# A graph layer's row gathers on GpSimd, issued in bursts of six that wait for TensorE's half groups

## The chip, the cores and the metric

The kernel is one program on one NeuronCore of a Trainium2 chip. The metric is the device time of one execution in microseconds (us); the time before is 13074.31 us, the median of three runs (13063.61 to 13083.32).

## The reference

The program computes nine layers on 32 sequences of 242 tokens with 64 features: a windowed token mixer, four attention layers and four feed-forward layers. The change touches only the last one, the graph layer, which treats all 7744 tokens as nodes of a graph with 262144 edges plus one loop per node:

```
h = (x_flat @ W_gat).reshape(M, HEADS, NUM_EXPERTS)      # 4 heads x 4 experts
a_src = (h * att_src).sum(-1); a_dst = (h * att_dst).sum(-1)
e = leaky_relu(a_src[src] + a_dst[dst], 0.2)
ee = exp(e - segment_max(e, dst)[dst])
alpha = ee / (segment_sum(ee, dst)[dst] + 1e-16)
agg = segment_sum(h[src] * alpha, dst) + b_gat
# layer norm, mean over heads, top 2 of 4 experts, and
out = sum over experts of gate * (gelu(x @ W1 + b1) @ W2 + b2)
```

What matters here is `h[src]` and `a_src[src]`: each of the 262144 edges needs the 20-number row (80 bytes) of its source node.

## The kernel before

In an earlier layer the edges are sorted by target node, so that each of the 128 partitions holds 2048 consecutive edges. The stage in question works through them in 16 chunks of `W = 128` edges per partition. For the edges of a chunk there are two ways to get the source rows:

- **Gathered.** The first `FETCHED = 72` edges of each partition come by indirect DMA: GpSimd issues one gather per edge column, 128 rows of 80 bytes each, from the table in device memory into `g_got` (L2829). That is 72 gathers per chunk and 1152 in all. Chunk `i` writes buffer `i % 3`.
- **Looked up.** The other 56 edges come in seven groups of eight by matrix products. ScalarE starts the DMA that lays the node numbers out (L2932), VectorE turns them into one-hot matrices (`mark`, L3001 and L3002), TensorE multiplies them with the table (`look`, L2861, in two halves of 24 matrix products), VectorE masks the product (`clear`, L3009, "g_picked"), TensorE folds it (`fold`, L2874) and ScalarE copies the rows out (`take`, L2954).

There are therefore 16 x 7 = 112 lookup groups, numbered G; the chunk is G // 7. TensorE does, for each G, the first half of the look of G, then the fold of G - 1, then the second half of the look of G. Two of its steps raise the semaphore `tensor_step` (looked up and folded): the fold of G brings it to 2G + 2, the second half of the look of G to 2G + 1. So it goes up by one per half of a group. VectorE's `clear` waits for the look, ScalarE's `take` for the fold, TensorE's fold for `clear`, and the look of G for the masking of G - 2. Also on TensorE in the same order are the small expert layers (L2838, L2845, L2854), two sequences per chunk, and before a fold in two of seven groups it waits for ScalarE's copy L2937.

VectorE's work on the finished rows of a chunk (`messages`) is cut into five pieces. From G = 16 on, one piece stands behind each group. The pieces of chunk `i` run, once the start is over, at G = 7(i + 1) + 1 to 7(i + 1) + 5. The second piece waits for the chunk's gathers (L3077), the fourth (L3095, "msg") reads `g_got` for the last time.

GpSimd's order is written out in one loop over chunks (L2811). Before chunk `i >= 3` it waits until VectorE's "msg" of chunk `i - 3` has freed the buffer, and then issues all 72 gathers in a run. In chunk 0 two other pieces of work stand between the gathers: 62 gathers of sorted keys (L2822), each waiting for a buffer that VectorE counts (L3026), ahead of gather 24, and 61 scatters of head values (L2827) ahead of gather 40. Chunks 1 and 2 wait for nothing.

Of the kernel before, what the change touches and what calls it, by code (L numbers as in the profile page):

```python
# [33 lines left out]
class Chain:  # L34
# [14 lines left out]
    def after(self, i, name):  # L49

        return i * self.per + self.end[name]
# [2442 lines left out]
def stage_l3_ffn(nc, h, xn, k, A):  # L2494
# [30 lines left out]
    with ExitStack() as outer:  # L2525
# [8 lines left out]
        with ExitStack() as edges:  # L2534
# [213 lines left out]
            PER = 7  # L2748
            MADE = GROUP * PER
            FETCHED = W - MADE  # L2750
            GROUPS = CHUNKS * PER
            with ExitStack() as ctx:
# [41 lines left out]
                vector_step, tensor_step, taken = sem("marked_and_cleared"), sem("looked_up_and_folded"), sem("rows_taken")  # L2794
# [3 lines left out]
                ch = Chain([sem("step")], ["fill", "weighed", "alpha", "sum", "leaky", "top", "diff", "gone", "fade", "exp", "msg", "run"])  # L2798
                s, after = ch.sem[0], ch.after
                SEARCH, SCATTER = 24, 40  # L2800
                PIECES, FIRST = 5, 2 * PER + 2
                slots, at_piece = [[] for _ in range(GROUPS)], 0
                for G in range(GROUPS):
# [5 lines left out]
                with nc.Block() as block:  # L2809
                    @block.gpsimd  # L2810
                    def _(g):  # L2811
                        for i in range(CHUNKS):
                            c = i % SLOTS
                            if i >= SLOTS:
                                g.wait_ge(s, after(i - SLOTS, "msg"))
                            for w in range(FETCHED):
                                if (i, w) == (0, SEARCH):
                                    g.wait_ge(ps_, pl("block_i"))
                                    for t in range(NODES + 1):
                                        if t >= RING:  # L2820
                                            g.wait_ge(near_used, t - RING + 1)
                                        g.indirect_dma_start(near[t % RING], None, ordered.rearrange("(n w) -> n w", w=BLK), bass.IndirectOffsetOnAxis(  # L2822
                                            ap=blk[:, t:t + 1].bitcast(U32), axis=0)).then_inc(near_in[t % RING], 16)
                                if (i, w) == (0, SCATTER):
                                    g.wait_ge(ps_, pl("place_i"))
                                    for t in range(NODES):
                                        g.indirect_dma_start(heads_at, bass.IndirectOffsetOnAxis(ap=place_i[:, t:t + 1].bitcast(U32), axis=0),  # L2827
                                                             brow[:, t, :], None).then_inc(heads_out, 16)
                                g.indirect_dma_start(got[c][:, w, :], None, rows, bass.IndirectOffsetOnAxis(  # L2829
                                    ap=idx[:, i * W + w:i * W + w + 1].bitcast(U32), axis=0)).then_inc(gathered[c], 16)  # L2830
# [679 lines left out]
```

## Time and profile before

| | |
|---|---|
| median of three runs | 13074.31 us |
| profiled execution, first to last instruction | 13092.4 us |
| TensorE busy | 10580.0 us (81%) |
| VectorE busy | 8992.0 us (69%) |
| ScalarE busy | 5348.0 us (41%) |
| GpSimd busy | 1494.4 us (11%), of it 1149.0 us in the 1152 gathers |
| TensorE's mean granted clock | 0.886 of full speed |

No other time of the profiled execution is given than its span; the profile has no time around it. Shares are means over nine very different layers, so they say little of one stage. The 112 lookup groups lie from about 10000 us to 12886 us of the span. A row of a timeline gives the start, the length, the engine and the line, and in brackets how long the engine had been idle before it and what ended that; "issue" is idle time in which the engine waited for nothing that the profile shows, "remote" that the releaser is not told.

### The profile page before, as it was taken

Reading aid. Unit: us, or ns where it says so; the run is one execution under the profiler, and the core shown is the slowest. Engines: PE = TensorE matmul, PEld = TensorE weight load, DVE = VectorE, ACT = ScalarE, POOL = GpSimd, SP = SyncE. Lnnn points to the kernel's source line nnn. Section 1 sums busy time; section 2 is a strip of 40 time slices with the busy share of each in tenths; the row PEclk is TensorE's granted clock in tenths of the full one; section 3 lists DMA queues with packets and bytes.
Section 4 is the critical chain, followed back from the end, with each engine's and each line's share of the span. In section 5 each row is a group of like instructions: output and inputs, shape, how many; then the busy total and the mean of one; then the engine's idle time right before and its main releaser. Section 6 shows DMA issues by size and latency. Waiting matters only on the chain. (4 is left out here: it accounts for less than half of the span.)

```text
span 13092.4 us, 170810 instructions
## 1 busy us (share of the span) xinstructions
PE 10580.0 (81%) x48685; PEld 6876.2 (53%) x48685; DVE 8992.0 (69%) x31958; ACT 5348.0 (41%) x12854; POOL 1494.4 (11%) x1505
## 2 busy tenths in 40 slices
PE   2597799996694999999999999999896356666663
PEld 2486577774583555555555555555695133333331
DVE  7777687775676888888888888887666123333335
ACT  2364356563352555555555555555452000000000
POOL 0000000000000000000000000000001644543442
PEclk6798799997896999999999999999897677777776
DMA  0000012110001444344444444444002522322222
GB/s 5 11 1 6 27 47 61 51 56 3 2 1 30 99 103 98 98 103 98 98 103 98 98 103 98 98 103 99 28 1 63 41 34 39 48 39 34 41 42 65
DMA packets 511176, 744.96 MB, mean 57 GB/s; under 512 B 183149, under 2 KB 423246, under 8 KB 489577
## 3 DMA queue, kind: packets, MB, share of 16 engines
q1 hardware_dynamic: 398623, 601.80, 18.6%
q0 software_dynamic: 76960, 65.91, 4.0%
q10 hardware_dynamic: 34688, 66.66, 2.1%
q8 instruction: 387, 6.34, 0.2%
q14 instruction: 518, 4.24, 0.1%
HBM read 459.00 MB, written 84.54 MB: 42 GB/s over the span
## 5 line engine op out<-in xcount | busy, mean ns | idle before, releaser
L1849 PE MATMUL pm_out<-pm_w,pm_tab 128*128 128x484 f32 x8192 | 3997.3, 569 | 0.2 <-DVE pm_w L2093 0.2
L1954 ACT ACTIVATE pm_e<-pm_sums 128x484 f32<-128x484 f32 x4096 | 2316.2, 573 | 1375.1 <-PE pm_sums L1864 1342.9
L2093 DVE SCALAR_TENSOR_TENSOR pm_w<-pm_sums,pm_e 128x484 f32<-128x484 f32 x4096 | 2660.9, 651 | 85.3 <-ACT pm_e L1954 68.9
L1849 PEld LDWEIGHTS pm_out<-pm_w,pm_tab 128*128 128x128 f32 x8192 | 1558.7, 191 | 1008.9 <-issue 733.6
L1864 PE MATMUL pm_sums<-pm_mv,pm_pick 96*128 96x484 bf16 x4096 | 1508.9, 369 | 20.4 <-DMA pm_mv<-pm_parts 20.4
L3009 DVE TENSOR_TENSOR g_picked<-g_lookup,g_mask 128x1024 f32<-128x1024 f32 x112 | 137.1, 1224 | 1797.4 <-PE g_lookup L2861 1008.7
L2829 POOL DMA_INDIRECT g_got<-gat_sources,ed_idx x1152 | 1149.0, 997 | 1269.8 <-DVE g_msg L3095 912.8
L2861 PE MATMUL g_lookup<-g_onehot,ed_parts 121*128 121x512 bf16 x2688 | 710.9, 410 | 432.7 <-issue 391.5
L2861 PE MATMUL g_lookup<-h,ed_parts 121*128 121x512 bf16 x2688 | 693.9, 410 | 221.4 <-issue 218.8
L2954 ACT ACTIVATE g_got<-g_ps 128x128 f32<-128x128 f32 x112 | 31.0, 277 | 2044.5 <-PE g_ps L2874 794.7
L1864 PEld LDWEIGHTS pm_sums<-pm_mv,pm_pick 96*128 96x128 bf16 x4096 | 408.9, 100 | 650.2 <-issue 405.5
L2861 PEld LDWEIGHTS g_lookup<-g_onehot,ed_parts 121*128 121x128 bf16 x2688 | 272.4, 103 | 837.7 <-issue 545.3
L2874 PE MATMUL g_ps<-ed_folds,g_picked 128*128 128x16 f32 x1792 | 258.2, 279 | 467.0 <-issue 261.6
L114 POOL TENSOR_TENSOR xn<-h,s_st 121x1024 f32<-121x1024 f32 x1 | 2.9, 2938 | 5208.0 <-DVE s_st L95 5208.0
L2861 PEld LDWEIGHTS g_lookup<-h,ed_parts 121*128 121x128 bf16 x2688 | 276.6, 105 | 603.8 <-issue 349.7
L936 ACT ACTIVATE a_s<-a_ps,a_nmax,a_rms 121x121 f32<-121x121 f32 (+1 forms) x1024 | 459.0, 503 | 177.6 <-DVE a_nmax L1018 176.7
L2874 PEld LDWEIGHTS g_ps<-ed_folds,g_picked 128*128 128x128 f32 x1792 | 271.3, 226 | 477.1 <-issue 335.5
L2039 DVE MAX8 pm_srt<-pm_sim 121x8 f32<-121x64 f32 x2880 | 475.2, 214 | 5.2
L863 PEld LDWEIGHTS a_pv<-a_vs,a_pT 121*121 121x121 f32 x3072 | 407.9, 187 | 21.6 <-ACT a_pT L942 1.0
L854 PE MATMUL a_ps<-a_kd,a_y 128*121 128x121 f32 (+1 forms) x2048 | 404.1, 320 | 0.0
L863 PE MATMUL a_pv<-a_vs,a_pT 121*121 121x65 f32 x3072 | 386.3, 262 | 0.9 <-DVE a_acc L1034 0.9
L2042 DVE MATCH_REPLACE8 pm_sim<-pm_srt,pm_sim 121x64 f32<-121x64 f32 x1920 | 386.5, 211 | 0.0
(595 smaller groups left out, 19254.8 us busy)
## 6 DMA issues: line engine op xcount, KB each, us to landing
pm_tab<-in_L_ffn_tables SPq DMA_DIRECT2D x128, 2048.0 KB, 8.0
pm_mv<-pm_parts SPq DMA_DIRECT2D x3072, 60.5 KB, 2.4
g_spread_low<-gat_low_and_high_rows ACTq DMA_DIRECT2D x112, 512.0 KB
pm_gb<-pk_threshold_rows SPq DMA_DIRECT2D x128, 242.0 KB, 7.6
gat_running<-g_rec SPq DMA_DIRECT2D x16, 1536.0 KB
g_got<-gat_sources,ed_idx POOLq DMA_INDIRECT x1152
gat_bounce<-a_keys SPq DMA_DIRECT2D x70, 256.0 KB
gat_bounce<-a_keys POOLq DMA_DIRECT2D x70, 256.0 KB, 4.7
```

Of the source, the lines that this page charges most:

```text
L854: ins = pe.matmul(S[0:TP, n % 2, KEYS[t]], y[n % 2][:, t * TP:(t + 1) * TP], kd[c][:, 0:(t + 1) * TP], start=False, stop=(t == NT - 1))
L863: ins = pe.matmul(PV[0:TP, at:at + V1], pT[n % 2][:, b, :], vs[c][:, j, n, :], start=(j == 0), stop=(j == t))
L936: ins = a.activation(s[n % 2][:, KEYS[t]], S[0:TP, n % 2, KEYS[t]], ACT.Exp, bias=nmax[n % 2][:, t:t + 1], scale=rms[c][:, t, n:n + 1])
L1849: pe.matmul(out[:, hd % 2, 0:CHUNK], tab[hd % 2][:, t, :], w[:, t % NW, :], start=(t == 0), stop=(t == KT - 1)).then_inc(used, 1)
L1864: pe.matmul(sums[:, t % NB, 0:CHUNK], pick[:, t % 2, :], mv[hd % 2][:, t // 2, :], start=True, stop=True).then_inc(sums_ready, 1)
L1954: a.activation(e[:, t % NW, :], sums[:, t % NB, 0:CHUNK], ACT.Exp).then_inc(exp_ready, 1)
L2039: ins = v.max(srt[:, n // 2, n % 2, r8:r8 + 8], x)
L2042: ins = v.match_replace(x, srt[:, n // 2, n % 2, r8:r8 + 8], x, NEG)
L2093: v.scalar_tensor_tensor(out=w[:, t % NW, :], in0=sums[:, t % NB, 0:CHUNK], scalar=0.0, in1=e[:, t % NW, :], op0=ALU.is_gt, op1=ALU.mult). ...
L2829: g.indirect_dma_start(got[c][:, w, :], None, rows, bass.IndirectOffsetOnAxis(ap=idx[:, i * W + w:i * W + w + 1].bitcast(U32), axis=0)).th ...
L2861: ins = pe.matmul(lookup[G % 2][:, half, :], parts[q][:, l, :, :].rearrange("k f i -> k (f i)"), onehot[G % ONEHOTS][:, l, half * BANK:(ha ...
L2874: ins = pe.matmul(ps[:, 0, at:at + HE], picked[G % 2][:, w * 128:(w + 1) * 128], folds[:, 0:HE], start=True, stop=True)
```

## The change

GpSimd's run of 72 gathers is cut into 12 bursts of six (`BURST = 72 / 14` rounded up). From chunk 1 on, before burst `b` of chunk `i`, GpSimd waits until `tensor_step` is at least 14(i - 1) + b, that is, until TensorE is through `b` half groups of the chunk before. The wait for 0 (chunk 1, burst 0) is left out. The wait for the free buffer stays, and so do all other engines' programs.

```
@@ -2798,6 +2798,7 @@
                 s, after = ch.sem[0], ch.after
                 SEARCH, SCATTER = 24, 40
+                BURST = -(-FETCHED // (2 * PER))
                 PIECES, FIRST = 5, 2 * PER + 2
@@ -2814,6 +2815,10 @@
                             if i >= SLOTS:
                                 g.wait_ge(s, after(i - SLOTS, "msg"))
                             for w in range(FETCHED):
+                                if i and w % BURST == 0:
+                                    half = 2 * PER * (i - 1) + w // BURST
+                                    if half:
+                                        g.wait_ge(tensor_step, half)
                                 if (i, w) == (0, SEARCH):
```

## Rows read from the trace of the kernel before

**Rows 1.** Costliest groups of the page: busy us, mean ns | idle before, releaser.

```profile
L3009 DVE TENSOR_TENSOR g_picked<-g_lookup,g_mask 128x1024 f32<-128x1024 f32 x112 | 137.1, 1224 | 1797.4 <-PE g_lookup L2861 1008.7
L2829 POOL DMA_INDIRECT g_got<-gat_sources,ed_idx x1152 | 1149.0, 997 | 1269.8 <-DVE g_msg L3095 912.8
```

**Rows 2.** Stretches of the stage: us, busy of PE, PEld, DVE, ACT, POOL, clock, DMA.

```profile
10593.00:12883.00 2290.00, 1521.42 (x7126) 810.09 (x7124) 791.12 (x1633) 131.64 (x245) 935.49 (x936) 0.77 0.25 42
...
10593.00:10700.00 107.00, 107.00 (x590) 62.15 (x589) 51.14 (x104) 10.26 (x19) 0.00 (x0) 1.00 0.15 45
10269.00:10593.00 324.00, 73.97 (x214) 28.65 (x213) 15.19 (x32) 2.34 (x6) 222.69 (x228) 0.53 0.30 15
```

**Rows 3.** Slices of 12 us from the start of one run of gathers.

```profile
12095.00:12107.00 12.00, 12.00 (x70) 6.89 (x70) 7.46 (x18) 0.28 (x1) 9.53 (x9) 1.00 0.47 52
12107.00:12120.00 13.00, 12.51 (x67) 6.41 (x64) 4.87 (x13) 0.28 (x1) 9.98 (x10) 1.00 0.64 178
12120.00:12132.00 12.00, 3.13 (x13) 2.41 (x13) 4.07 (x9) 0.00 (x0) 9.26 (x10) 0.59 0.33 20
...
12168.00:12180.00 12.00, 2.34 (x4) 0.51 (x5) 0.00 (x0) 0.00 (x0) 9.08 (x10) 0.50 0.22 8
...
12204.00:12216.00 12.00, 12.00 (x66) 7.14 (x65) 4.78 (x10) 1.25 (x2) 0.00 (x0) 1.00 0.18 44
```

**Rows 4.** Timeline of GpSimd: first, slowest and last gather of that run.

```profile
12094.92 1.04 POOL L2829 DMA_INDIRECT g_got<-gat_sources,ed_idx  x1 [82.04 <-DVE g_msg L3095]
...
12130.85 2.07 POOL L2829 DMA_INDIRECT g_got<-gat_sources,ed_idx  x1 [0.30 <-issue]
...
12186.90 0.94 POOL L2829 DMA_INDIRECT g_got<-gat_sources,ed_idx  x1 [0.31 <-issue]
```

**Rows 5.** Timeline of TensorE before, in and after that run.

```profile
12076.21 3.57 PE L2874 MATMUL g_ps<-ed_folds,g_picked 128*128 128x16 f32 x16 [6.59 <-ACT ed_xT L2937]
12079.62 7.78 PE L2861 MATMUL g_lookup<-g_onehot,ed_parts 121*128 121x512 bf16 x24
...
12107.76 1.86 PE L2874 MATMUL g_ps<-ed_folds,g_picked 128*128 128x16 f32 x16
12109.47 5.34 PE L2861 MATMUL g_lookup<-g_onehot,ed_parts 121*128 121x512 bf16 x24
...
12129.07 2.31 PE L2874 MATMUL g_ps<-ed_folds,g_picked 128*128 128x16 f32 x10 [8.26 <-issue]
...
12164.20 0.58 PE L2861 MATMUL g_lookup<-h,ed_parts 121*128 121x512 bf16 x1 [2.21 <-issue]
```

**Rows 6.** Timeline: steps of VectorE and ScalarE that TensorE releases, in that run.

```profile
12101.14 1.22 DVE L3009 TENSOR_TENSOR g_picked<-g_lookup,g_mask 128x1024 f32<-128x1024 f32 x1 [4.41 <-issue]
...
12114.31 0.28 ACT L2954 ACTIVATE g_got<-g_ps 128x128 f32<-128x128 f32 x1 [18.09 <-remote]
...
12127.79 1.23 DVE L3009 TENSOR_TENSOR g_picked<-g_lookup,g_mask 128x1024 f32<-128x1024 f32 x1 [15.93 <-remote]
...
12196.45 0.28 ACT L2954 ACTIVATE g_got<-g_ps 128x128 f32<-128x128 f32 x1 [81.86 <-remote]
```

**Rows 7.** Timeline of VectorE: the picks of G = 11, 103, 110 and 111.

```profile
10593.33 1.22 DVE L3009 TENSOR_TENSOR g_picked<-g_lookup,g_mask 128x1024 f32<-128x1024 f32 x1 [51.11 <-PE g_lookup L2861]
...
12766.48 1.23 DVE L3009 TENSOR_TENSOR g_picked<-g_lookup,g_mask 128x1024 f32<-128x1024 f32 x1 [4.41 <-PE g_lookup L2861]
...
12868.86 1.23 DVE L3009 TENSOR_TENSOR g_picked<-g_lookup,g_mask 128x1024 f32<-128x1024 f32 x1 [4.40 <-PE g_lookup L2861]
...
12882.57 1.22 DVE L3009 TENSOR_TENSOR g_picked<-g_lookup,g_mask 128x1024 f32<-128x1024 f32 x1 [6.78 <-PE g_lookup L2861]
```

**Rows 8.** Stretches within the first run of 72: until and from its first late step.

```profile
10705.00:10744.00 39.00, 39.00 (x214) 22.14 (x212) 28.67 (x63) 2.34 (x6) 30.39 (x26) 1.00 0.43 101
10744.00:10802.00 58.00, 19.30 (x64) 7.42 (x63) 8.13 (x18) 1.56 (x2) 44.25 (x46) 0.58 0.23 17
```

**Rows 9.** Timeline at the end of the longest run: last gather, ScalarE's next step.

```profile
10559.88 1.00 POOL L2829 DMA_INDIRECT g_got<-gat_sources,ed_idx  x1 [0.30 <-issue]
...
10588.37 0.28 ACT L2954 ACTIVATE g_got<-g_ps 128x128 f32<-128x128 f32 x1 [47.91 <-remote]
```

**Rows 10.** The stretch of the paced key gathers.

```profile
10082.00:10204.00 122.00, 106.61 (x491) 58.96 (x492) 77.17 (x192) 6.25 (x14) 59.64 (x62) 0.86 0.52 164
```

**Rows 11.** Timeline of GpSimd: one pause among the key gathers.

```profile
10104.53 0.94 POOL L2822 DMA_INDIRECT g_rec<-gat_ordered,g_blk  x1 [4.64 <-DVE g_weighed L3026]
```

More of the change, by code:

```diff
@@ L2800, in stage_l3_ffn @@
                 SEARCH, SCATTER = 24, 40
+                BURST = -(-FETCHED // (2 * PER))
                 PIECES, FIRST = 5, 2 * PER + 2
@@ L2816, in _ @@
                             for w in range(FETCHED):
+                                if i and w % BURST == 0:
+                                    half = 2 * PER * (i - 1) + w // BURST
+                                    if half:
+                                        g.wait_ge(tensor_step, half)
                                 if (i, w) == (0, SEARCH):
```

## The prediction

> **What bounds the kernel now.** I read the page's costliest groups first, then stretches of the graph stage, then one run of gathers engine by engine. In the groups, VectorE's pick sits idle 1797.4 us before its 112 executions, mostly until TensorE's look, and GpSimd sits idle 912.8 us of its 1269.8 us before the gathers until "msg" frees a buffer [rows 1]. So GpSimd isn't short of time, and VectorE waits for TensorE. One would say that TensorE bounds the stage. But in the 2290 us from G = 11 to G = 111 it is busy only 1521.42 us, at 0.77 of its clock, while in the 107 us without a gather it is busy all the time at 1.00 [rows 2].
>
> The slices over one run of gathers show where the rest goes. Two slices after the run's start TensorE still executes 70 and 67 products; then 13, and further on 4 per slice, at clock 0.50; once the gathers are over, 66 again [rows 3]. The gathers go from 12094.92 to 12186.90 at an even step (0.94 us and 0.30 us of issue; 2.07 us was the slowest) [rows 4]. TensorE's rows say how it is slowed: a half group of 24 products takes 5.34 us, in the run single products come 2.8 us apart (0.58 and 2.21 of "issue") though nothing in the program stands between them [rows 5]. And what TensorE tells others comes late: the fold that ends at 12109.62 is acted on by ScalarE at 12114.31, the look that ends at 12114.81 is seen by VectorE at 12127.79, and ScalarE's next step comes 81.86 us after its last, at 12196.45, 8.6 us after the last gather's end [rows 4 to 6]. That late signal, not the arithmetic, sets the stage's pace.
>
> The cost of it: picks G = 103 to 110, with no gather beside them, take 12868.86 - 12766.48 = 102.38 us for seven groups, that is 1462.6 us for a hundred. G = 11 to 111 took 12882.57 - 10593.33 = 2289.24 us [rows 7]. The excess is 826.6 us, over the 936 / 72 = 13 runs of that stretch [rows 2]: **63.6 us a run**. Before them, 61 scatters and 167 of the 176 gathers that follow them without a pause fill 324 us in which TensorE gets through three groups (about 44 us worth) [rows 2]; the time there is GpSimd's own.
>
> **The change part by part.**
>
> *Waits added.* 15 chunks x 12 less one = 179 waits on GpSimd. Nothing is queued behind a waiting gather but gathers. VectorE needs chunk i's rows in its second piece, at G = 7(i + 1) + 2; the last burst is let go at half 14(i - 1) + 11, in group 7(i - 1) + 5. That leaves over ten groups, 150 us at the undisturbed pace, for at most 7.5 us of gathers. The lateness costs nothing. The buffer is free in time: "msg" of chunk i - 3 is at G = 7(i - 2) + 4, three groups ahead of burst 0. The waits' own time is on an engine that idles 912.8 us [rows 1]: 0.
>
> *Gathers moved.* They now stand beside groups 7(i - 1) to 7(i - 1) + 5 and no longer run on while TensorE stands still. I reckon with GpSimd's step of 0.94 + 0.30 = 1.25 us [rows 4]: a burst takes 7.5 us, a half group of TensorE 102.38 / 14 = 7.3 us on average, 6.9 us when nothing waits (5.34 + 1.86 less overlap) [rows 5, 7]. So the bursts do NOT make pauses at full pace. They follow each other nearly without one, 90 us of gathers in 12 halves of 88 us. What they do is to tie GpSimd to the very signal that comes late: when tensor_step is late by some us, GpSimd stops after at most six gathers.
>
> *What TensorE then loses.* How long a run is harmless I take from rows: in one run the first 39 us cost nothing (TensorE busy 39.00 of 39.00 at clock 1.00), and the next 58 us cost most (19.30 of 58.00) [rows 8]; in the other the first signal was late 15 us in and the first idle time came at 26 us [rows 3 to 6]. So 25 us on average, then GpSimd is held. After a last gather it takes 8.6 us until signals come through [rows 4, 6]; TensorE has some 5 us of other work (a half, 5.34 us [rows 5]) meanwhile, so it idles about 4 us. It may lose its clock over that: after 6.59 us idle the fold took 3.57 instead of 1.86 us and the half 7.78 instead of 5.34 us, 4.1 us in all [rows 5]. So 8 us a hold. One pause is there anyway, where TensorE waits 6.59 us for ScalarE in each chunk. 90 us of gathers with it make two holds a chunk: **16 us a run** in place of 63.6. Gain 13 x 47.6 = 619 us. Bounds: below, the holds stay within TensorE's slack and cost 0 (gain 826.6); above, 63.6 as now (gain 0), and beyond it the rival of the other sign. I take 16 since it is nearest to the paced key gathers: 62 in 122 us, with pauses like 4.64 us, beside which TensorE was busy 106.61 of 122 us [rows 10, 11]. These were half as dense, so something above nothing is left.
>
> *The start.* The scatters, the last 32 gathers of chunk 0 and all of chunk 1 still go in one run, since halves 1 to 11 are long past: (61 + 104) x 1.27 = 210 us. Chunk 2 may at once have the halves up to about 21, eight bursts, and only some 24 of its 72 gathers are put off: 30 us of GpSimd's run. The signals come back after it in proportion: 28.5 us after the longest run [rows 9], 8.6 after 92 us. Gain 30 to 40 us, less the hold of the put-off ones: **30 us**, bounds 0 and 90 (the whole of chunk 2, if the halves 15 to 21 are seen late).
>
> Sum: 619 + 30 = 649 us. From the profiled span, 13092.4 - 649 = 12443. The page gives no time around the span, and the median of the runs is 18.1 us under it, so I take 18 off: **12425 us**.
>
> *A rule against it.* The rows show that TensorE's rate falls to a fifth and less while GpSimd gathers [rows 3]. The Trainium skill, "SBUF — State Buffer", section "SBUF: two separate sides", says that engine ports and DMA ports are disjoint and that a DMA can't be slowed by a compute operation, nor the other way round; by that alone the place of the gathers would not matter and the time would stay 13074. The trace speaks against applying it here, since the slowdown starts and ends with the gathers.
>
> **The rivals.**
>
> *A. GpSimd holds itself back so early that TensorE hardly notices.* The first late signal is only 4.7 us late [rows 5, 6], and GpSimd would stop on it before TensorE idles. For it: the key gathers [rows 10]. Against it: pauses there came every nine gathers, here they come only once something is late. 3 us a run, gain 13 x 60.6 + 30 = 818: 12256 us.
>
> *B. The drain isn't complete when the late signal arrives.* Then the next burst soon makes TensorE late again, six holds of 8 us instead of two, 48 us a run. For it: the bursts leave no idle time of their own. Gain 13 x 15.6 + 30 = 233: 12841 us.
>
> *C. The cost belongs to each gather, wherever it stands,* or GpSimd never really waits, and the runs stay in one piece. 63.6 us a run whatever the order: 13074, or 13044 with the start's gain. Against it: 39 us of gathers that cost nothing [rows 8].
>
> *D. The other side: a burst of six is enough to stop TensorE's signals, and GpSimd and TensorE go by turns.* Then every burst costs its 7.5 us and the 8.6 us of drain ahead of the next half, with the half's own 7.3 us beside one of them only: 12 x (7.5 + 8.6) + 14.6 = 208 us a chunk, against 102.38 + 63.6 = 166 now. That is 42 us more in 13 runs, 546 us, so 13620 us. It decides from the point where signals are late within the first 7.5 us of a run. Against it: nothing was late in the first 12 us of these rows [rows 3, 6].
>
> **How the numbers follow.** My forecast 0.47, A 0.22, B 0.18, C 0.06, D 0.07. Its own range is 12330 to 12600 (one to four holds). The range goes from 12200 (just under A) to 12880 (just over B); C, D and a little at both ends are outside. Within 0.2% (26 us, about what a measurement of this kernel can tell) lies only part of C: 0.04. Slower is D and a rest: 0.07. Faster 0.89.
>
> **What would show it.** In the changed profile: gathers in the stage in stretches well under 72, with GpSimd's idle time ahead of them ended by TensorE's look and fold, not by "msg"; no idle time over some 15 us between TensorE's products from G = 12 on, and no row of single products 2.8 us apart for 60 us; a TensorE clock above 0.77 in the stage; picks of G = 12 to 111 about 13.7 us apart with a few at 20 to 25; seven groups in some 118 us. Wrong it would be if the runs are whole (C), if the picks all lie 25 us or more apart (D), or if the groups' period falls but something else, as VectorE's wait for the gathers at L3078, appears in its place. The layers before this one must not move.

## The result and the profile after

The changed kernel takes 12522.58 us (median of four, 12483.97 to 12533.41) against 13069.33 us for the kernel before (median of four; one run more than in the 13074.31 above): ratio 0.9568, 95% interval 0.9549 to 0.9588. The forecast was 12425 us, range 12200 to 12880. The profiled execution of the changed kernel spans 12482.2 us, 610.2 us less than before, and is the fastest of its four; the medians are 547 us apart.

The page's two groups, to be laid beside [rows 1] (busy us, mean ns | idle before it, releaser):

```profile
L2834 POOL DMA_INDIRECT g_got<-gat_sources,ed_idx x1152 | 1219.4, 1059 | 691.0 <-issue 345.7
L3014 DVE TENSOR_TENSOR g_picked<-g_lookup,g_mask 128x1024 f32<-128x1024 f32 x112 | 137.1, 1225 | 1198.9 <-remote 598.5
```

VectorE's idle time before its picks fell by 598.5 us (1797.4 - 1198.9), which is nearly all of the 610. GpSimd's fell too, and "msg" is no longer what it mostly waits for. What it waits for between G = 11 and G = 111 is the view of waits from 10540 to 12270 us (us in total, times, longest):

```profile
POOL g_got L2834 <- issue: 287.7, 915, 7.6
POOL g_got L2834 <- DVE g_msg L3100: 152.7, 4, 85.9
POOL g_got L2834 <- PE g_ps L2879: 104.3, 16, 11.3
POOL g_got L2834 <- remote: 38.2, 14, 5.1
POOL g_got L2834 <- PE g_lookup L2866: 19.6, 11, 2.5
```

So "msg" holds back four runs in place of 13, all before G = 35, and the new waits (fold, look and "remote") add up to 162.1 us in 41 holds (a "remote" one may still be "msg"). Stretches, as in [rows 2] (us; busy of PE, PEld, DVE, ACT, POOL; clock; DMA share and GB/s): first G = 11 to 111, then a part without many gathers, then G = 8 to 11, and last the two parts of the first, G = 21 to 35 and G = 35 to 111:

```profile
10549.00:12272.00 1723.00, 1426.29 (x7124) 786.18 (x7122) 792.33 (x1633) 131.88 (x245) 1027.34 (x955) 0.88 0.32 56
10549.00:10655.00 106.00, 106.00 (x584) 61.26 (x583) 50.73 (x103) 10.27 (x19) 19.30 (x19) 1.00 0.19 47
10255.00:10549.00 294.00, 70.91 (x218) 29.11 (x217) 15.37 (x33) 2.35 (x6) 202.51 (x210) 0.54 0.29 16
...
10680.00:11024.00 344.00, 215.27 (x994) 114.22 (x992) 122.33 (x250) 20.55 (x36) 210.88 (x206) 0.76 0.28 46
11024.00:12272.00 1248.00, 1080.02 (x5415) 597.07 (x5413) 599.60 (x1238) 100.16 (x187) 782.38 (x718) 0.90 0.34 59
```

TensorE executes the same 7124 products in 1723 us instead of 2290, at clock 0.88 instead of 0.77. The picks of G = 11, 21, 35 and 111 on VectorE's timeline divide it up:

```profile
10548.86 1.23 DVE L3014 TENSOR_TENSOR g_picked<-g_lookup,g_mask 128x1024 f32<-128x1024 f32 x1 [17.66 <-issue]
...
10679.54 1.23 DVE L3014 TENSOR_TENSOR g_picked<-g_lookup,g_mask 128x1024 f32<-128x1024 f32 x1 [0.61 <-issue]
...
11024.21 1.23 DVE L3014 TENSOR_TENSOR g_picked<-g_lookup,g_mask 128x1024 f32<-128x1024 f32 x1 [2.03 <-PE g_lookup L2866]
...
12271.73 1.23 DVE L3014 TENSOR_TENSOR g_picked<-g_lookup,g_mask 128x1024 f32<-128x1024 f32 x1 [6.78 <-PE g_lookup L2866]
```

With the undisturbed 102.38 / 7 = 14.63 us a group [rows 7], the excess from G = 35 to 111 is 1247.52 - 1111.6 = 135.9 us for ten runs, **13.6 us a run** (before: 1761.88 - 1111.6 = 650.3, 65.0 a run). From G = 21 to 35 it is 344.67 - 204.8 = 139.9 us for the runs of chunks 3, 4 and 5: **46.6 us a run** (before: 396.67 us in all, 64.0 a run). The next rows show a hold at work, in the timeline of one chunk:

```profile
11614.06 0.95 POOL L2834 DMA_INDIRECT g_got<-gat_sources,ed_idx  x1 [1.89 <-PE g_lookup L2866]
...
11622.01 0.28 ACT L2959 ACTIVATE g_got<-g_ps 128x128 f32<-128x128 f32 x1 [4.90 <-PE g_ps L2879]
...
11633.82 1.86 PE L2879 MATMUL g_ps<-ed_folds,g_picked 128*128 128x16 f32 x16
...
11640.59 0.28 ACT L2959 ACTIVATE g_got<-g_ps 128x128 f32<-128x128 f32 x1 [18.31 <-remote]
...
11644.12 1.10 PE L2866 MATMUL g_lookup<-g_onehot,ed_parts 121*128 121x512 bf16 x4 [0.50 <-issue]
...
11649.07 1.10 PE L2866 MATMUL g_lookup<-g_onehot,ed_parts 121*128 121x512 bf16 x4 [1.72 <-issue]
...
11657.56 1.23 DVE L3014 TENSOR_TENSOR g_picked<-g_lookup,g_mask 128x1024 f32<-128x1024 f32 x1 [22.76 <-remote]
11657.79 0.95 POOL L2834 DMA_INDIRECT g_got<-gat_sources,ed_idx  x1 [3.41 <-remote]
```

The fold that ends at 11635.68 (11633.82 + 1.86) is acted on 4.9 us late, and from 8.4 us after its end TensorE executes its products in small clusters with "issue" between them. GpSimd stops for the half that doesn't arrive, and 3.41 us later VectorE and GpSimd go on together. The same state lasted some 70 us in the run of before [rows 3, 6].

The change makes this lateness short; it doesn't remove it. I add up, from G = 35 on, how late a fold or look reached a partner that stood waiting for it (the start of ScalarE's or VectorE's step less the end of TensorE's, which is modelled): 621 us in the kernel before, 58.7 us the longest, 16 of them over 10 us; in the changed kernel 296 us, 18.2 us the longest, 7 over 10 us.

### The profile page after: what moved, and what is told of

The parts are those of the page before. It is cut to its first block and busy times, and to the rows that moved or that the text cites. A ratio compares the mean times of both kernels' runs of the same rounds, so it can differ in the third digit from the quotient of the medians.

```text
span 12482.2 us, 170823 instructions
## 1 busy us (share of the span) xinstructions
PE 10484.1 (84%) x48685; PEld 6853.3 (55%) x48685; DVE 8994.2 (72%) x31958; ACT 5358.8 (43%) x12854; POOL 1566.2 (13%) x1505
## 3 DMA queue, kind: packets, MB, share of 16 engines
q0 software_dynamic: 76960, 65.91, 4.0%
## 5 line engine op out<-in xcount | busy, mean ns | idle before, releaser
L2834 POOL DMA_INDIRECT g_got<-gat_sources,ed_idx x1152 | 1219.4, 1059 | 691.0 <-issue 345.7
L3014 DVE TENSOR_TENSOR g_picked<-g_lookup,g_mask 128x1024 f32<-128x1024 f32 x112 | 137.1, 1225 | 1198.9 <-remote 598.5
L2866 PE MATMUL g_lookup<-g_onehot,ed_parts 121*128 121x512 bf16 x2688 | 664.3, 400 | 178.2 <-issue 139.0
L2866 PE MATMUL g_lookup<-h,ed_parts 121*128 121x512 bf16 x2688 | 660.3, 399 | 80.7 <-issue 79.6
```

Of the source, the lines that this page charges most:

```text
L2866: ins = pe.matmul(lookup[G % 2][:, half, :], parts[q][:, l, :, :].rearrange("k f i -> k (f i)"), onehot[G % ONEHOTS][:, l, half * BANK:(ha ...
```

## The experiments

In all of them "excess" is the time from the pick of G = 35 to that of G = 111 less 1111.6 us, divided by the ten runs in it. The kernel before took 13069 us on the chip of the first measurement and 13147 to 13203 us in the sets below, so ratios to the kernel before of the same set are compared. Even they carry some 0.6% between sets: the changed kernel came out at 0.9568 and at 0.9511, and these intervals don't overlap. One wait a chunk, bursts of five, the chunks 3 to 5 and the memset of 1 are one set, without the changed kernel; changed again, bursts of 24, the paced kernel and the memset of 256 are a second; the memsets of 128 and of 192 and the change with 192 are a third; half the rows is a fourth.

| kernel | us | ratio (95%) | G 8 to 11 | G 11 to 21 | G 21 to 35 | excess a run |
|---|---|---|---|---|---|---|
| before (first profile) | 13069.33 | 1 | 324.9 | 130.7 | 396.7 | 65.0 |
| changed (first profile) | 12522.58 | 0.9568 (0.9549 to 0.9588) | 294.1 | 130.7 | 344.7 | 13.6 |
| changed, again | 12560.11 | 0.9511 (0.9495 to 0.9527) | 290.0 | 146.6 | 371.3 | 15.6 |
| one wait a chunk | 13210.11 | 1.0052 (1.0032 to 1.0072) | 325.0 | 131.9 | 389.6 | 77.0 |
| bursts of five | 12475.36 | 0.9499 (0.9483 to 0.9514) | 280.6 | 134.0 | 349.1 | 11.8 |
| bursts of 24 | 12801.40 | 0.9702 (0.9685 to 0.9718) | 296.6 | 161.2 | 390.9 | 35.4 |
| chunks 3 to 5 later | 12485.33 | 0.9505 (0.9489 to 0.9520) | 289.6 | 136.3 | 291.3 | 18.8 |
| paced from the start | 12300.91 | 0.9322 (0.9306 to 0.9337) | 59.0 | 212.9 | 273.6 | 15.6 |
| before + memset of 1 | 13133.27 | 0.9989 (0.9980 to 0.9999) | 281.5 | 163.1 | 387.7 | 70.5 |
| before + memset of 128 | 13020.02 | 0.9864 (0.9847 to 0.9880) | 282.6 | 161.8 | 377.4 | 60.2 |
| before + memset of 192, scatters too | 12571.07 | 0.9520 (0.9504 to 0.9536) | 56.8 | 336.6 | 200.7 | 29.8 |
| before + memset of 256 | 12250.23 | 0.9281 (0.9265 to 0.9296) | 171.0 | 136.9 | 192.3 | 11.0 |
| changed + memset of 192, scatters too | 12402.24 | 0.9399 (0.9384 to 0.9415) | 57.8 | 339.5 | 217.5 | 18.1 |
| before, half the rows | 13294.59 | 1.0069 (1.0052 to 1.0086) | 326.3 | 213.8 | 353.5 | 80.1 |

**Is it the place or the holding?** One wait a chunk:

```
-                                if i and w % BURST == 0:
+                                if i and w == 0:
```

> Only the wait ahead of burst 0 of each chunk stays: the gathers stand where the change puts them, but as one run of 72. My theory (GpSimd must be held by the late signal, or pause, within 15 to 40 us): the excess is again about 63.6 us a run, so the time is near that of before, 13030 to 13090 us. Rival (the new place beside other groups is what helps, or TensorE's ScalarE wait falls better): near the changed kernel, 12480 to 12560 us.

GpSimd's waits in this kernel, from 10700 us of the span to G = 111:

```profile
POOL g_got L2834 <- PE g_ps L2879: 695.6, 8, 91.5
POOL g_got L2834 <- issue: 371.4, 924, 90.1
POOL g_got L2834 <- DVE g_msg L3100: 271.1, 4, 146.0
```

The start of each run was moved as the change moves it (up to 91.5 us of waiting for a fold), but the run stayed whole, and the time is 0.5% over that of before. It is 120 us above the window I had given, of which 77 us are the set's slower kernel before. The place does nothing for it: the excess is 77.0 us a run, against 65.0 before. The holding inside the run makes the gain.

**Shorter and longer bursts.** Bursts of five (`BURST = FETCHED // (2 * PER)`), and bursts of 24 (`BURST = 24`, waiting for halves 0, 4 and 8):

> Bursts of five, 15 a chunk, so that a burst takes 6.3 us and is shorter than an undisturbed half group of 6.9 us. My theory (a late signal needs gathers without a pause; with real pauses there is none): chunks 5 to 15 lose 0 to 5 us in place of about 14 us, so 12370 to 12450 us. Rival (each hold is inherent to a number of gathers, 72 a chunk whatever the pauses): as the changed kernel, within 30 us of 12520. Second rival (more waits, more holds): 12600 us and more.

> Bursts of 24 at halves 0, 4 and 8: 30 us of gathers, which no signal can stop, then a wait. By the rows a run is harmless for 15 to 39 us, and what is late comes through some 8.6 us after the last gather. My theory: three bursts a chunk each lose 0 to 15 us; the excess is 20 to 40 us a run, slower than the changed kernel by 50 to 250 us, still well under the kernel before. Rival (the length doesn't matter so long as there is some pause): within 30 us of the changed kernel.

The stretch G = 35 to 111, first of the bursts of five, then of those of 24, each from its own kernel:

```profile
11029.00:12259.00 1230.00, 1098.81 (x5412) 612.23 (x5410) 600.88 (x1238) 99.80 (x187) 776.98 (x723) 0.90 0.35 60
```

```profile
11111.00:12577.00 1466.00, 1164.19 (x5416) 606.81 (x5414) 599.63 (x1238) 100.03 (x187) 740.78 (x718) 0.84 0.29 50
```

Bursts of five left 11.8 us a run where I had expected 0 to 5, and their ratio overlaps that of the changed kernel run again. I wouldn't say that "real pauses" don't help: in the trace the gathers from chunk 7 on still come in stretches of up to 22 between idle times of over 1 us, since several halves are often past at once. A pause after every five wasn't made here. Bursts of 24 do what the length theory says: 35.4 us a run, inside 20 to 40, and 241 us over the changed kernel in the same set.

**The early chunks.** The halves of chunks 3, 4 and 5 moved on:

```
-                                    half = 2 * PER * (i - 1) + w // BURST
+                                    half = 2 * PER * (i - 1) + w // BURST + {3: 11, 4: 7, 5: 3}.get(i, 0)
```

> The changed kernel with the halves of chunks 3, 4 and 5 moved 11, 7 and 3 on, to where the free buffer lets them begin. In the changed kernel chunks 3 and 4 still run 72 gathers without a wait, since msg of the chunk three before comes so late at the start that all their halves are past. My theory: these two then cost some 15 us each in place of 59 and 43 us; gain 60 to 80 us, 12440 to 12465 us. Rival (chunk 3 and 4 are slow for another reason, such as the head and record transfers there): within 20 us of the changed kernel.

Stretches G = 21 to 35 and G = 35 to 111:

```profile
10679.00:10970.00 291.00, 214.24 (x975) 114.79 (x973) 123.06 (x250) 20.96 (x37) 204.13 (x196) 0.80 0.31 50
10970.00:12270.00 1300.00, 1117.15 (x5416) 616.24 (x5414) 600.32 (x1238) 99.99 (x187) 769.97 (x725) 0.88 0.33 57
```

The first stretch fell from 344 us (371 in the second profile) to 291, a gain of 53 to 80 us where I had forecast 60 to 80. So chunks 3 and 4 were slow because all their halves were past when their buffer came free. But the second grew from 1248 (1268) to 1300 us, and the ratio isn't distinguishable from the changed kernel's run again; the forecast 12440 to 12465 us for the whole kernel wasn't reached (12485.33). Why the later chunks went at 18.8 us a run here I can't say; the bursts settled into a steady pattern of 24 and 12, and which pattern arises differs from profile to profile.

**The start paced too.** The scatters and chunks 0 to 5 let go seven to a half, later chunks 5.4 to a half (`due(u) = 15 + u // 7` up to unit 453, then `80 + (u - 453) * 5 // 27`, a wait where it changes). The changed kernel ran in the same set.

> The changed kernel once more, beside the others of this set: the kernel before had 13069 us on one chip and 13147 us on another, so only ratios within a set can be compared. Every theory: ratio 0.950 to 0.960 to the kernel before.

> The 61 scatters, the last 32 gathers of chunk 0 and chunks 1 to 5 are let go seven to a half from half 15 on, and the later chunks 5.4 to a half, in place of six to a half from each chunk's own start. In the changed kernel G = 8 to 40 took 863 us, with 227 issues in nearly one piece and two whole runs of 72. Theory 'pace': GpSimd needs 453 x 1.27 = 575 us for all up to chunk 5, which lie now in 65 halves of some 8.9 us; G = 8 to 40 takes 560 to 660 us, and the later chunks go as with bursts of five. 200 to 300 us faster than the changed kernel, ratio to the kernel before 0.930 to 0.942. Rival 'the work is moved, not saved' (what stood in one run at the start costs the same later): within 60 us of the changed kernel, ratio 0.948 to 0.957.

G = 8 to 35, and G = 35 to 111:

```profile
10255.00:10800.00 545.00, 427.90 (x1926) 220.29 (x1925) 208.15 (x427) 34.15 (x64) 385.18 (x371) 0.82 0.34 49
10800.00:12068.00 1268.00, 1106.06 (x5416) 608.98 (x5414) 601.09 (x1237) 100.06 (x187) 846.17 (x793) 0.89 0.34 59
```

259 us faster than its neighbour, inside 200 to 300, all of it before G = 35 (808 us in the neighbour, 545 here).

**Is it the rate?** No wait on TensorE at all: the kernel before, and GpSimd does a memset after each gather. It waits for its memset before by a semaphore, except for the shortest, which writes another place each time.

```
+                                g.wait_ge(ready, 1 + i * FETCHED + w)
+                                g.memset(pad[:, :], 0.0).then_inc(ready, 1)
```

> The kernel before, with one small memset of GpSimd after each gather of the run, so that the step from gather to gather grows from 1.25 us to some 1.4 to 1.6 us; no wait on TensorE is added and each run stays whole. After a run of 92 us signals came through 8.6 us late, after one of 300 us 28.5 us late: the gathers ask for about 1.09 times what can be served. Theory 'rate': at a step of 1.4 us or more nothing is ever late, TensorE is undisturbed beside the run, the excess of 63.6 us a run goes to under 10, and the time is 12250 to 12450 us. Rival 'length' (a run without TensorE's own pauses is harmful at any step): 72 steps of 1.5 us take longer, the excess grows, and the time is 13100 to 13300 us.

> The kernel before, with a memset of 256 numbers a partition after each gather; the short one before fitted into the 0.3 us between two gathers and left the step at 1.25 us. The step is now some 1.4 to 1.7 us and each run whole. Theory 'rate' (the gathers ask for 1.09 times what can be served): nothing is late, the excess of 63.6 us a run goes to under 15, time 200 to 700 us under the kernel before. Rival 'length': a run of 72 x 1.5 us = 108 us hurts as long as it lasts, 100 to 250 us slower than the kernel before.

The shortest memset, timeline of GpSimd: it lies within the 0.3 us that were idle anyway, and the usual step stays 1.25 us (11572.67 to 11573.92), not the 1.4 us and more that I wanted. Averaged over whole runs (chunks 3 to 15, first to last gather) the step did grow, from 1.30 to 1.38 us, by single longer ones; the excess didn't fall (70.5 us a run). It is also the control for the memset itself.

```profile
11572.67 0.94 POOL L2830 DMA_INDIRECT g_got<-gat_sources,ed_idx  x1 [0.19 <-issue]
11573.62 0.12 POOL L2833 MEMSET g_pad<- 32x1 bf16 x1
11573.92 0.94 POOL L2830 DMA_INDIRECT g_got<-gat_sources,ed_idx  x1 [0.18 <-issue]
```

With 256 numbers, the same view: usual step 1.44 us, 1.54 on average.

```profile
11503.31 0.95 POOL L2830 DMA_INDIRECT g_got<-gat_sources,ed_idx  x1 [0.17 <-issue]
11504.24 0.34 POOL L2833 MEMSET g_pad<- 128x256 f32 x1
11504.75 0.95 POOL L2830 DMA_INDIRECT g_got<-gat_sources,ed_idx  x1 [0.17 <-issue]
```

Its stretch G = 21 to 111, and one row of its waits:

```profile
10572.00:11985.00 1413.00, 1215.46 (x6404) 694.89 (x6403) 818.98 (x1487) 120.18 (x222) 1263.79 (x1830) 0.92 0.36 63
```

```profile
DVE g_e L3081 <- DMA g_got<-gat_sources,ed_idx: 162.1, 11, 27.4
```

More work for GpSimd made the kernel 7.2% faster, 948 us, more than the 200 to 700 that I had expected, with no wait on TensorE in it. The lateness summed as above is 8 us from G = 35 on, 1.2 us the longest. Now VectorE waits for the gathers (162.1 us in 11 waits): seven groups take 110 to 112 us because 72 gathers do (72 x 1.54 = 111), not because a signal is late. It pays for that at the end: the last gather starts at 12038.8, after the pick of G = 111 (11985.4), and from that pick to the end of the span it takes 264 us in place of 210. This is still the fastest of all, 51 us under the paced kernel of its set and 310 us under the changed one. Two steps between:

> The kernel before with a memset of 128 numbers in place of 256 after each gather: a step of some 1.33 us (1.44 with 256, 1.25 with none or the shortest). Theory 'rate' with a limit near 1.36 us, as the late signals of 8.6 and 28.5 us gave: still a little too fast, signals late by 2% of a run's length, seldom; the excess is 0 to 20 us a run and the ratio to the kernel before 0.925 to 0.945. If the limit lies above 1.36 us: excess 30 us and more, ratio above 0.95. If it lies well below: seven groups in 102 to 106 us, ratio 0.920 to 0.926.

> The kernel before with a memset of 192 numbers after each gather and each of the 61 scatters: step some 1.39 us. Theory 'rate': no signal late, GpSimd needs 72 x 1.39 = 100 us a chunk, so seven groups take 103 to 107 us in place of 111; G = 8 to 11 falls from 171 us to under 80 us, but what is put off there is made up for in later groups. 40 to 120 us faster than with 256 numbers: ratio 0.918 to 0.926. Rival (GpSimd's own time is the bound at the start, nothing to gain by spacing the scatters): ratio 0.926 to 0.930.

> The changed kernel (bursts of six, waiting for the half groups) with the same memsets as the kernel beside it. Theory 'the change works only as a brake on the rate': with the rate already under the limit its waits add nothing; the time is that of its neighbour without them, or up to 60 us slower, since six in a half of 7.3 us is 8.3 us of GpSimd. Rival 'the tie to the half groups has a worth of its own': 20 us or more faster than its neighbour.

G = 35 to 111, with 128 numbers (usual step 1.34 us, 1.41 on average), then with 192 (1.39 us, 1.47 on average):

```profile
11082.00:12795.00 1713.00, 1195.23 (x5411) 617.80 (x5410) 615.75 (x1237) 99.84 (x187) 865.22 (x1434) 0.78 0.25 43
```

```profile
10853.00:12263.00 1410.00, 1138.88 (x5416) 617.39 (x5414) 654.74 (x1239) 100.07 (x187) 1025.96 (x1584) 0.88 0.32 53
```

Both of my numbers here were wrong. I had the limit at 1.36 us, from how late signals came after two runs [rows 6, 9]. But at 1.34 us the excess is still 60.2 us a run, and at 1.39 us 29.8; only at 1.44 us is it down to 11.0. So the limit lies between usual steps of 1.39 and 1.44 us, or average ones of 1.47 and 1.54. The average is partly an effect, since gathers take longer beside a busy VectorE: in the changed kernel 1.28 to 1.67 us from 11616 to 11623, while VectorE works, and 0.94 to 0.96 from 11636 to 11654, while it waits. The usual step is what one sets. With 192 numbers the unbroken stretch of scatters and gathers at the start still did harm, only later: G = 11 to 21 took 337 us, where the changed kernel took 131, but G = 8 to 11 took 57 in place of its 294. The change and the memset of 192 together are 1.3% faster than the memset alone (0.9399 to 0.9520 in one set), so the rival expectation held: at a rate still over the limit the holding helps. Over a step under the limit it wasn't tried.

**Per gather or per row?** The kernel before, gathering for 64 partitions; the rows of the others are left out.

```
-    g.indirect_dma_start(got[c][:, w, :], None, rows, ... ap=idx[:, ...]
+    g.indirect_dma_start(got[c][0:64, w, :], None, rows, ... ap=idx[0:64, ...]
```

> The kernel before, its gathers fetching the rows of 64 partitions instead of 128; the rows of the other 64 partitions are left out (zeros stand for them). The number of gathers and the runs of 72 stay. By the steps tried so far the limit lies between 1.39 and 1.44 us a gather of 128 rows. Theory 'rows' (what is short is spent per row): half the rows at a step not under 0.75 us stay below the limit, no fold is acted on late, the excess is under 10 us a run, and the 324 us of G = 8 to 11 fall too: ratio to the kernel before 0.90 to 0.93. Theory 'issues' (it is spent per gather, as its 16 increments of the semaphore are): if the step stays at 1.25 us, the lateness stays and the ratio is 0.98 to 1.01; if the step shrinks, it gets worse in the run but the run is shorter.

Timelines of GpSimd and of ScalarE:

```profile
11499.24 0.91 POOL L2829 DMA_INDIRECT g_got<-gat_sources,ed_idx  x1 [0.31 <-issue]
11500.45 0.90 POOL L2829 DMA_INDIRECT g_got<-gat_sources,ed_idx  x1 [0.30 <-issue]
```

```profile
11576.04 0.28 ACT L2954 ACTIVATE g_got<-g_ps 128x128 f32<-128x128 f32 x1 [80.40 <-remote]
```

The step is 1.21 us in place of 1.25, and with half the rows ScalarE still sits 80.40 us for a fold. The excess is 80.1 us a run, more than the 65.0 of before, perhaps because the step is shorter; that wasn't tried by itself. Here the theory "issues" foresaw a ratio of 0.98 to 1.01, and "rows" 0.90 to 0.93. So what runs out isn't spent per row or per byte. It isn't the time of the 16 DMA engines either: GpSimd's DMA queue took 20.0% of it in a run of the kernel before (12095 to 12187) and 7.1% in a run with half the rows (11494 to 11583). But one thing didn't change with the rows: the queue moved 76960 packets in both kernels, with 65.91 and with 60.01 MB in them. So "per gather" and "per packet of a gather" remain side by side. The Trainium skill, "DMA: Bandwidth & Descriptors", section "Anatomy of one DMA — SWDGE (gpsimd) path", counts a fixed part for each DMA issued by GpSimd that doesn't grow with its size; this agrees in kind, though the page says nothing of TensorE.

## Why the prediction was right

- *What bounds the stage* (late signals of TensorE, 63.6 us a run): right. Holding shortens the lateness, a longer step removes it (621, 296 and 8 us from G = 35 on), and the excess falls with it (65.0, 13.6 and 11.0, the last set by the gathers' own time). Pacing takes the time out of the start (808 to 545 us for G = 8 to 35). The place alone gains nothing.
- *Waits added, buffer in time, gathers early enough: 0.* Right for VectorE's need: in the changed kernel nothing waits for a gather. The buffer was in time only from chunk 6 on. At the start the messages run late (from G = 16), so "msg" of chunks 0 to 2 comes when the halves of chunks 3 to 5 are wholly or in part past. I had taken the steady state's three groups of room for all chunks. That is the term that I missed: 46.6 us a run in three runs in place of 16, 92 us. With these halves moved on, the stretch won 53 to 80 us, but the later chunks lost 32 to 52 of them again.
- *Two holds of 8 us, 16 us a run:* measured 13.6 us in the ten later runs. The product is right, its two factors aren't, and they make up for each other. GpSimd was held there 38 times by fold, look or "remote" (147.4 us, 3.9 on average), that is 3.8 times a run and not twice; 13.6 / 3.8 makes some 3.6 us of TensorE's time for each and not 8 (an estimate). By kind the kernel lies between my forecast and rival B. That the size came out is in part luck.
- *The thirteen runs together:* 20.0 us a run for 16, gain 566.4 us for 619.
- *The start: 30 us.* Measured 324.9 - 294.1 = 30.8 us, and by the way foreseen: the unbroken run of gathers after the scatters is 146 long in place of 176. One reading behind it was uneven: the 28.5 us after the longest run count from the start of its last gather [rows 9]; from its end, as the 8.6 us do, they are 27.5.
- *The sum:* 597 us by the picks and 610 in the span, for 649. The medians lie 63 us nearer to each other than the profiled spans do. I took one offset of 18 us for both; before, the profile lay 23 us over the median, after it lies 40 us under it. Of the changed kernel's four runs the profiled one is the fastest (12483.97; the others took 12521 to 12533), so a single profile is not exact here. Against the median the forecast gain of 649 us stands at 547.
- *A* (3 us a run) and *D* (turns, 13620 us) didn't come. *B*, an incomplete drain with 48 us a run, didn't come in size (13.6), though there were more holds than two. *C* was refuted by the change itself.
- *The signs.* Seen were holds by look and fold, a clock of 0.88, and 120.6 us for seven groups (for 118). Not seen, at the start: chunks 3 and 4 still ran as whole runs of 72, and TensorE once stood idle for 28.9 us between two products (until 10882), where I had allowed 15.
- *The rule on ports.* By the Trainium skill, "SBUF — State Buffer", section "SBUF: two separate sides", nothing would have moved. The runs decide against applying it: TensorE's rate depends on the step between gathers (excess 65 us a run at a usual step of 1.25 us, 11 at 1.44). No run here shows at which point the two meet, and the rule may well hold for the ports themselves.

## What to carry to other kernels

If an engine shows single instructions with "issue" between them and its partners wait on "remote", look for a stream of small DMAs that starts and ends with it, and ask for the rate of that stream before its place. Holding the issuer by a signal that comes late under the load is a brake that sets itself, but each run must really meet the wait: check the start-up chunks, where another wait decides when the run begins. A fixed, slightly longer step can do better than the brake, and it is the cheaper experiment: one idle instruction after each DMA, long enough to lengthen the step. Read the step from the trace, the usual one and the average.

## What the hardware showed

- Indirect DMAs from GpSimd at a step of 1.25 us slowed TensorE's single instructions to one in 2.8 us and delayed what it told ScalarE by up to 88 us (the fold of G = 9 in the kernel before ended at 10381.2 and was taken at 10469.2), though the 16 DMA engines were busy only 0.22 of the time at the slowest [rows 3]. The harm was 65, 60, 30 and 11 us a run at usual steps of 1.25, 1.34, 1.39 and 1.44 us: most of the fall lies between 1.34 and 1.44.
- Half the rows in each gather hardly changed the step (1.21 us), didn't lessen the harm (80 us a run), and left the number of packets as it was.
- A GpSimd memset of 0.12 us fits between two gathers and leaves the usual step at 1.25 us. Behind one of 0.34 us another 0.17 us stay idle, and the step is 1.44 us.
- What is behind it stays open: which part of the chip serves both the gathers and TensorE's signals, whether it counts gathers or their packets, and whether fewer packets a gather would help, was not tried.
